# A decoder block in float32: VectorE's slot list reordered, and the order of the feed-forward's first projections

## The reference

```python
x = x + attn(layernorm(x), wq, wk, wv, wo)      # 32 heads of 16, 8 key heads, causal
x = x + xattn(layernorm(x), ctx, mask, Wq, Wk, Wv, Wo, q_norm_w, k_norm_w)
x = x + ffn(layernorm(x), gate_w, up_w, down_w, fc1_w, fc2_w, expert_w, gamma, beta)

def xattn(h, c, mask, ...):                     # 32 heads of 128, 8 key heads
    q, k, v = h @ Wq.T, c @ Wk.T, c @ Wv.T
    q, k = rmsnorm(q, q_norm_w), rmsnorm(k, k_norm_w)
    p = softmax(q @ k.T / sqrt(128) + mask)
    return (p @ v) @ Wo.T

def ffn(h, ...):
    top2 = sum(top_k(h @ gate_w, 2))
    shared = (relu(h @ up_w) ** 2) @ down_w
    routed = (((h @ fc1_w) @ expert_w) * top2) @ fc2_w
    return layernorm(shared + routed, gamma, beta)
```

## Time and profile before

| | |
|---|---|
| median of 3 runs | 1743.43 us (1742.48 to 1743.58) |
| the profiled execution | 1742.22 us |
| its span, first to last instruction | 1740.5 us |
| TensorE, matmuls | 1644.4 us busy, 94% |
| VectorE | 1153.2 us, 66% |
| ScalarE | 760.8 us, 44% |
| GpSimd | 658.1 us, 38% |
| mean granted clock of TensorE | 0.989 of full |
| DMA queues | 12.9% of 16 engines' time; 512 KB pieces land 3.7 us after their issue |

### The profile page before, as it was taken

How to read it: one execution, slowest core, us unless ns; L and a number is a source line. 1 busy time by engine, 2 the same in 40 slices (tenths; PEclk the granted TensorE clock), 3 DMA queues, 4 the chain that set the end, 5 groups by cost and what they waited for, 6 DMA issues and landing times.

```text
span 1740.5 us, 40966 instructions
## 1 busy us (share of the span) xinstructions
PE 1644.4 (94%) x16856; PEld 1338.8 (77%) x16856; DVE 1153.2 (66%) x1977; ACT 760.8 (44%) x1396; POOL 658.1 (38%) x511
## 2 busy tenths in 40 slices
PE   5999899999999999989988999999999999998898
PEld 4566787878888788778865567887878778786797
DVE  4488767676766676874545877676675767668643
ACT  2575535344444444431226744445353544444221
POOL 3596423333233332460126944243232332335400
PEclk9999999999999999999999999999999999999999
DMA  4110012021020120211111101020120210201000
GB/s 171 59 43 1 24 40 63 2 63 45 20 63 20 44 69 1 62 61 38 58 62 50 31 1 57 7 63 20 44 63 2 63 44 20 69 20 56 19 19 25
DMA packets 26215, 73.04 MB, mean 42 GB/s; under 512 B 3120, under 2 KB 3376, under 8 KB 26032
## 3 DMA queue, kind: packets, MB, share of 16 engines
q1 hardware_dynamic: 26032, 70.22, 12.9%
HBM read 66.01 MB, written 4.19 MB: 40 GB/s over the span
## 4 chain that ended last, share of the span: by engine, by line
PE 62%; issue 15%; DVE 11%; POOL 9%; ACT 2%; DMA 1%; POOLq 0%; SPq 0%; DVEq 0%; ACTq 0%
PE acc L407 10%; PE acc L408 9%; PE acc L409 9%; PE y L407 8%; PE y L409 7%; PE y L408 7%; POOL w_lo L1654 4%; PE quad L672 4%; POOL prob L1667 2%; PE quad L701 2%; POOL prob L1673 2%; PE quad L588 2%; DVE pmax L1247 1%; DVE w_lo L1188 1%; PE y L685 1%
## 5 line engine op out<-in xcount | busy, mean ns | idle before, releaser
L407 PE MATMUL y<-w_hi 128*128 128x512 f32 x576 | 235.6, 409 | 34.8 <-POOL w_lo L1654 17.1
L1667 POOL TENSOR_TENSOR prob<-prob,pmax 128x512 f32<-128x512 f32 x128 | 135.9, 1062 | 277.6 <-DVE pmax L1247 277.2
L407 PE MATMUL acc<-w_hi,xn_hi 128*128 128x512 f32 (+1 forms) x576 | 227.6, 395 | 11.2 <-DVE xn_lo L1188 11.2
L1673 POOL TENSOR_TENSOR prob<-prob,prec 128x512 f32<-128x512 f32 x128 | 148.4, 1159 | 231.2 <-DVE prec L1255 231.2
L408 PE MATMUL y<-w_lo,w_hi 128*128 128x512 f32 x576 | 227.2, 394 | 0.0
L409 PE MATMUL y<-w_hi,w_lo 128*128 128x512 f32 x576 | 227.1, 394 | 0.0
L408 PE MATMUL acc<-w_lo,xn_hi 128*128 128x512 f32 (+1 forms) x576 | 221.1, 384 | 0.0
L409 PE MATMUL acc<-w_hi,xn_lo 128*128 128x512 f32 (+1 forms) x576 | 219.3, 381 | 0.0
L1264 DVE TENSOR_TENSOR x<-y,x 128x512 f32<-128x512 f32 x144 | 99.3, 689 | 177.3 <-PE y L409 177.3
L1658 POOL TENSOR_TENSOR qkrs<-qkve,mhalf 128x10 f32<-128x10 f32 x64 | 124.9, 1952 | 230.1 <-DVE qkve L1339 230.1
L1654 POOL TENSOR_TENSOR w_lo<-stage,w_hi 128x1024 fp32r<-128x1024 f32 (+1 forms) x88 | 170.4, 1945 | 90.9 <-ACT w_hi L852 90.9
(11 more groups left out here) (129 smaller groups left out, 3780.3 us busy)
## 6 DMA issues: line engine op xcount, KB each, us to landing
stage<-in_w_cross SPq DMA_DIRECT2D x64, 512.0 KB, 3.7
stage<-in_w_cross SPq DMA_DIRECT2D x32, 256.0 KB, 3.3
stage<-in_w_ffn SPq DMA_DIRECT2D x16, 512.0 KB, 3.6
x<-in_x SPq DMA_DIRECT2D x8, 512.0 KB, 4.2
stage<-in_w_self SPq DMA_DIRECT2D x8, 512.0 KB, 4.4
kt<-in_ctx SPq DMA_DIRECT2D x16, 256.0 KB, 2.9
out_x<-x SPq DMA_DIRECT2D x16, 256.0 KB, 2.0
stage<-in_w_self SPq DMA_DIRECT2D x4, 256.0 KB, 3.7
```

The lines of the kernel that those rows point to most:

```text
L407: nc.tensor.matmul(target, l_hi, r_hi, start=first, stop=False)
L1667: nc.gpsimd.tensor_tensor(pr, pr, spread(pmax[:, buffer, :], 8, SEQ), ALU.subtract).then_inc(s_sub.sem, 1)
L1673: nc.gpsimd.tensor_tensor(pr, pr, spread(prec[:, buffer, :], 8, SEQ), ALU.mult).then_inc(s_nrm.sem, 1)
```

## The change

No instruction is added or removed. On VectorE, in every slot and in the last turn, the softmax sum and `outputs_lo` go ahead of the transposes. On ScalarE `sibling_keys` goes between the two query copies. At the end of the last turn `updated(3)`, `outputs_lo(3)` and several steps of the feed-forward's first quarter are moved. On TensorE the transpose of tile 4 goes between the last two output blocks, and `up(0, 2)` and `up(0, 3)` go ahead of `latent(1)`; `FFN` numbers the banks accordingly.

```diff
--- before.py
+++ after.py
@@ -53,7 +53,7 @@
 C_KV, C_Q = 0, 1
 EARLY = {name: n for n, name in enumerate(
     ["lx5", "lx6", (1, C_KV), (1, C_Q), (1, C_Q + 1), (2, C_KV), (2, C_Q), (2, C_Q + 1), "lx7"])}
-FFN = ("ln0 ln1 lat00 lat01 ln2 ln3 up00 up01 latt0 ln4 ln5 lat10 lat11 up02 up03 ln6 ln7 latt1 "
+FFN = ("ln0 ln1 lat00 lat01 ln2 ln3 up00 up01 latt0 ln4 ln5 up02 up03 lat10 lat11 ln6 ln7 latt1 "
        "up10 up11 up12 up13 lat20 lat21 latt2 up20 up21 up22 up23 lat30 lat31")
 SELF_END = "kt0 kt1 q4 q5 q6 q7 lx0 lx1 lx2 lx3 lx4 ckv cq0 cq1"
 FIRST = ("*ln0 *ln1 *kv0 *ln2 *ln3 *kv1 *ln4 *ln5 *kv2 *ln6 *ln7 *kv3 "
@@ -808,12 +808,12 @@
                 up(0, 1)
                 transpose_latent(0)
                 outputs(turn, 3, 0)
+                norm(4)
                 outputs(turn, 3, 1)
-                norm(4)
                 norm(5)
-                latent(1)
                 up(0, 2)
                 up(0, 3)
+                latent(1)
                 down(0, 0)
                 norm(6)
                 down(0, 1)
@@ -1078,11 +1078,11 @@
                 exps(at, k + 1, (k + 1) % PRING)
                 keys_and_values(place, k + 3)
                 outputs_hi(at, k)
-                sibling_keys(at, k + 2)
                 if next_group and k == 0:
                     split_piece(place, 6)
                     split_piece(place, 7)
                 queries(place, k + 3, 0)
+                sibling_keys(at, k + 2)
                 queries(place, k + 3, 1)
                 if next_group and k == 0:
                     split_piece(place, 8)
@@ -1142,13 +1142,13 @@
                 rectify(0, 1)
                 latent_hi(0)
                 split_piece(place, 6)
+                norm_hi(4)
 
                 act.wait_ge(y_rdy.sem, at(y_rdy, 0))
                 split_piece(place, 7)
+                norm_hi(5)
                 hidden_hi(0, 0)
-                norm_hi(4)
                 hidden_hi(0, 1)
-                norm_hi(5)
                 rectify(0, 2)
                 hidden_hi(0, 2)
                 rectify(0, 3)
@@ -1450,10 +1450,10 @@
                 masked_scores(at, k + 1)
                 row_max(at, k + 1, (k + 1) % PRING)
                 scale_chunk(at, k + 2)
+                sums(at, k + 1, (k + 1) % PRING)
+                outputs_lo(at, k)
                 transposed(place, k + 2)
-                sums(at, k + 1, (k + 1) % PRING)
                 key_squares(place, k + 3)
-                outputs_lo(at, k)
                 query_squares(place, k + 3, 0)
                 query_squares(place, k + 3, 1)
                 variance(at, k + 3)
@@ -1538,10 +1538,10 @@
                 masked_scores(turn.at, 1)
                 row_max(turn.at, 1, 1)
                 scale_chunk(turn.at, 2)
+                sums(turn.at, 1, 1)
+                outputs_lo(turn.at, 0)
                 transposed(turn, 2)
-                sums(turn.at, 1, 1)
                 key_squares(turn, 3)
-                outputs_lo(turn.at, 0)
                 query_squares(turn, 3, 0)
                 query_squares(turn, 3, 1)
                 variance(turn.at, 3)
@@ -1563,10 +1563,10 @@
                 final_statistics(2)
                 outputs_lo(turn.at, 2)
                 latent(0)
+                updated(3)
                 norm(2)
                 masked_scores(turn.at, 3)
                 row_max(turn.at, 3, 3)
-                updated(3)
                 final_statistics(3)
                 sums(turn.at, 3, 3)
                 norm(3)
@@ -1577,26 +1577,26 @@
                 final_statistics(5)
                 norm_lo(3)
                 norm(4)
+                outputs_lo(turn.at, 3)
                 norm(5)
                 square(0, 0)
-                outputs_lo(turn.at, 3)
                 square(0, 1)
                 latent_lo(0)
                 updated(6)
+                norm_lo(4)
                 updated(7)
+                norm_lo(5)
                 hidden_lo(0, 0)
-                norm_lo(4)
                 hidden_lo(0, 1)
-                norm_lo(5)
                 final_statistics(6)
-                final_statistics(7)
-                latent(1)
-                norm(6)
-                norm(7)
                 square(0, 2)
                 hidden_lo(0, 2)
+                final_statistics(7)
+                norm(6)
                 square(0, 3)
                 hidden_lo(0, 3)
+                norm(7)
+                latent(1)
                 norm_lo(6)
                 result(0)
                 norm_lo(7)
```

## The result

The changed kernel takes 1725.28 us, the median of four runs (1722.86 to 1727.11), beside 1743.51 us for the kernel before in the same comparison. The ratio is 0.9895 with a 95% interval of 0.9878 to 0.9912, so it is 1.05% faster. The forecast was 1722.9 us with a range of 1715 to 1735. The profiled execution took 1727.06 us (before: 1742.22), 15.2 us less where the sum said 20.5.

The account below looks back on a forecast made before the run. TensorE, busy 94% of the span, was taken to bound the kernel, so only its pauses and low-clock stretches could give. 6.9 + 2 x (1.1 + 5.7) = 20.5 us off 1743.43 gave 1722.9 us, range 1715 to 1735.

Parts of the forecast that it names:

- Part 1: Slot 0 of each half's first turn: sums and `outputs_lo` ahead of the transposes shorten TensorE's pause, 3.45 us each.
- The 1.57 us of clock: Slot 0 of a first turn: its 24 matmuls run at full clock behind the shorter pause, 7.25 to 5.68 us.
- The cover that was named in the last turn: Last turn: slack before the scores for later transposes and sibling copies is thinnest; loss 0 to 0.5 us per half, taken as 0.
- The transposes beside GpSimd's splits: VectorE's slot 0: transposes now beside GpSimd's splits would not stretch, or the cover would hold; effect 0.
- Part 2: Six later turns of each half: the pause is TensorE's own instruction stream returning after the jump; gain 0.
- Part 3: End of last turn: update 3 ahead of norm 2 and mask delays the softmax; loss 0.6 us, overtaken in Part 4.
- At 1.9 us the clock may fall: Pause ahead of the last transpose of probabilities: lower clock behind it taken as 0, bound 1.5 us per half.
- Part 4: Third chunk's output block: `outputs_lo(3)` ahead of norm 5 ends TensorE's wait for it; net gain 1.1 us per half.
- Part 5: Feed-forward start: two up projections ahead of the second latent one remove its 3.84 us wait and low clock; 5.7 us per half.
- the margin that I called my thinnest: First down projection: the fourth hidden part is ready near 772, TensorE uses it from 772.9; margin 0.9 us.
- the rival of the half-kept feed-forward: Fourth hidden part comes late, `down(0, 0)` waits: loss of 3 to 5 us per half, 1729 to 1733; chance 0.18.
- The new wait ahead of `up(0, 3)`: Feed-forward start: TensorE arrives before GpSimd ends piece 7; a new wait of about 0.5 us.

Follow-up runs that it names:

- low part 3 alone: The kernel before with only `outputs_lo(3)` moved ahead of `norm(5)` on VectorE: 1740.17 us, ratio 0.9978.
- the written-out one: The kernel before with TensorE's loop of seven turns written out and nothing else: 1733.41 us, ratio 0.9943.
- the slot order alone: The kernel before with only VectorE's sums and `outputs_lo` ahead of the transposes, `sibling_keys` left in its old place: 1738.38 us, ratio 0.9977.
- the experiment with the low part 1 moved ahead: The changed kernel with `outputs_lo(1)` also moved ahead of `scale_chunk(3)` in the last turn: 1722.89 us, ratio 0.9882.
- The written-out kernel: The changed kernel with TensorE's loop of seven turns written out, the other engines keeping their loops: 1701.39 us, ratio 0.9768.

## Why the prediction was right, and where a term was off

**Part 1, first turns: right.** 3.45 us were forecast for each. The pauses fell from 2.92 and 2.46 us to 0.96 and 0.62, and slot 0 runs at 1.00. From the profile, 286.53 - 285.07 + 2.24 = 3.70 us in half 0, and 3.80 in half 1, with 0.14 and 0.36 of it from a shorter return of the second turn. The 1.57 us of clock in this term are partly luck: behind the same wait the clock didn't fall in half 1 of two other runs of the old order (2.56 us in the run with low part 3 alone, 3.04 in the written-out one), so there the part would have been worth its 1.9 us alone. The cover that was named in the last turn (0 to 0.5 us) held only because `sibling_keys` moved too; without that move the slot order alone shows 0.94 us.

**The transposes beside GpSimd's splits: right that nothing comes of it.** VectorE's slot 0 in the changed kernel:

```profile
209.38 3.43 DVE L1351 TENSOR_TENSOR qb<-qb,qkrs 128x1024 f32<-128x1024 f32 x1
...
212.73 0.67 DVE L1252 TENSOR_REDUCE psum_<-prob 128x8 f32<-128x512 f32 x1
...
213.56 1.20 DVE L1188 TENSOR_TENSOR w_lo<-quad,w_hi 128x1024 fp32r<-128x1024 f32 x1
214.68 0.43 DVE L1237 STREAM_TRANSPOSE kt<-kv 128x256 f32<-128x256 f32 x1
215.04 1.26 DVE L1241 STREAM_TRANSPOSE qb<-qb 128x512 f32<-128x512 f32 x2
```

GpSimd has a split from 214.72 to 217.27, and the three transposes end at 215.04 + 1.26 = 216.30, 1.62 us after their start. In the kernel before they took 1.63 us with GpSimd idle, two of them again 1.26. The scaling, with two SBUF operands, takes 3.43 us here, beside a split, and 1.22 in the experiment with the low part 1 moved ahead, where it lay beside none.
The Trainium skill (GPSIMD Engine Reference, 1. Specifications) names VectorE instructions with two SBUF inputs or in a 2-port mode as those that contend with GpSimd. The trace agrees for the scaling (3.43 us) and for the transposes, which have one input (1.26 us). No trace shows which instruction runs in a 2-port mode.

**Part 2, later turns: right**, and this is the part on which most hung. The low part now ends at 281.11 + 1.20 = 282.31, 2.8 us ahead of TensorE's start at 285.07, and the pause is still 1.11 us. That refutes VectorE's low part. It doesn't refute the releaser that the view names, GpSimd's split: its pair ends at 284.80, 0.27 us ahead of TensorE's start. The written-out kernel does, where TensorE starts before that pair has ended, and it shows the return. What I hadn't seen is what the return covered: 0.6 us of VectorE's lateness in every turn.

```profile
281.11 1.20 DVE L1188 TENSOR_TENSOR w_lo<-quad,w_hi 128x1024 fp32r<-128x1024 f32 x1
```

**Part 3, update 3 first: the mechanism was right, one term was mis-sized.** The pause of "about 1.9 us" is 1.95 and 1.94, and the transpose came 0.6 us later against the end of the output block behind the last turn's pause (16.35 to 16.93 us). But the step "At 1.9 us the clock may fall ... 0, bound 1.5 us per half" held in half 1 only: in half 0 the clock fell to 0.77, and 0.9 us were lost. The value was picked as the nearer of two rows, 1.82 and 2.46. The premise, that the length of a pause decides between them, is wrong: the clock fell behind one pause of 1.81 us and not behind another, and it fell in five of the ten of 1.90 to 1.97 us. So the better value was about half of what a fall costs, 0.45 us per half.

**Part 4, low part 3 early: right**, 1.8 us at the output block in both halves when made alone. With part 3 in front, outputs(3, 0) starts 1.2 us earlier in half 1, counted from the end of the output block behind the last turn's pause (27.07 to 25.89 us), where 1.1 were forecast. In half 0 it is only 0.3 (27.10 to 26.80 us): that is the 0.9 us of clock of part 3.

**Part 5, up projections first: right.** 5.7 us were forecast. From outputs(3, 0) to the transpose of norm 6 it was 28.18 us and is 775.33 - 752.74 = 22.59, so 5.6, and the same in half 1. VectorE's timeline: norm 4, now alone ahead of the low part, then that low part, then the fourth hidden one:

```profile
746.50 2.76 DVE L1208 TENSOR_SCALAR xn<-x,mv,rstd 128x512 f32<-128x512 f32 x1
...
750.57 1.23 DVE L1188 TENSOR_TENSOR w_lo<-quad,w_hi 128x1024 fp32r<-128x1024 f32 x1 [1.31 <-ACT w_hi L1064]
...
769.43 1.02 DVE L1188 TENSOR_TENSOR w_lo<-qb,w_hi 128x512 fp32r<-128x512 f32 x1 [0.69 <-ACT w_hi L1113]
```

The low part is there at 751.80 (forecast 752.3), and TensorE, starting at 752.74, doesn't wait for it. The fourth hidden part ends at 770.45 (forecast: near 772), and TensorE's first matmul on it starts at 772.60, so the margin that I called my thinnest was 2.1 us and not 0.9, and the rival of the half-kept feed-forward had nothing to stand on. The new wait ahead of `up(0, 3)` was 0.36 us where 0.5 were forecast.

**The sum.** By the stretches it is 3.7 + 3.8 + 5.9 + 6.8 = 20.2 us, and 20.5 were forecast. The rest of the distance in the profiled execution, 5 us, lies in openings that the change doesn't touch, and comes and goes between executions of the same kernel. That the sum came so close is partly luck, since each of its terms of clock can be there or not in one execution.

## What to carry to other kernels

A wait's named releaser is a guess where the engine has just jumped back: compare the end of the releaser's instruction with the start of the waiter's, in a turn that was jumped to and in one that wasn't. If the distances differ (0.93 and 0.13 us here), suspect the jump, and settle it by writing the loop out. Write out such a loop on the engine that bounds the kernel first, since the jump (here 20 us of 1743) also hides what a reordering is worth. When work is moved ahead of other work to remove one pause, add up the pauses that it merges: 0.74 and 0.39 us were harmless, the pause of 1.9 us that took their place cost the clock too in half of the cases. And read each stretch in both halves of a program: what half 0 shows of the clock need not hold in half 1.

## What the runs showed of the hardware

- The return of TensorE's loop stands for 1.0 to 1.8 us and differs from turn to turn in one execution; with the restart a turn loses 1.7 us (20.7 / 12). Three of them, of 1.80, 1.81 and 1.84 us, had a granted clock of 0.77 behind them; another of 1.81 us had 1.00.
- The length of a pause alone doesn't tell whether TensorE's granted clock falls behind it. The shortest with a fall was 1.80 us. The clock stayed up behind pauses of 1.94 us (changed kernel, half 1), 2.36 (low part 1 early, half 0), 2.56 and 3.04 us (first turn of half 1 in two runs).
- The granted clock of one and the same kernel moved between 0.988 and 0.994 over its executions, and its time with it, 1727.4 to 1721.9 us. That is more than the interval of a single comparison (0.9878 to 0.9912 is 6 us wide) lets one see in a part worth 1 or 2 us, so such parts were read from stretches.
- A normalisation with one tensor operand is stretched beside GpSimd's splits (2.76 us for 512 columns, and 0.54 at 751.71 of the changed kernel with GpSimd idle), while transposes are not (1.26 us for two, beside a split and without), nor is a row sum of 512 columns (0.67 us at 216.52 beside a split, 0.64 in the kernel before with GpSimd idle).
